# A mixture-of-experts layer with its second shared products moved, a 14-slot weight ring, and expert rows scattered into a table by token and choice

## The chip, the core and the metric

One core of a Trainium2 chip runs one program. The metric is the device time of one execution in microseconds. TensorE (PE) multiplies, VectorE (DVE) and ScalarE (ACT) work element by element, GpSimd (POOL) does so too and issues the indirect transfers, and SyncE (SP) issues the plain transfers. All transfers run on the core's 16 DMA engines.

## What is computed

The input x is 32 x 32 x 512, read as 1024 tokens (rows) of 512. Two layers are added to it, one after the other; the change touches the first and the seam between them.

```python
# first layer
xt = einsum(x, weights[condition])                # a 32x32 mix per batch row -> 1024 x 512
scores = softmax(xt @ router_w + router_b) + router_bias
idx = top 2 experts of 16, within the best 2 groups of 4
gate[t, idx] = scores[t, idx]
y = sum over e of gate[:, e] * ((silu(xt@w1[e]+b1[e]) * (xt@w2[e]+b2[e])) @ w3[e] + b3[e])
z = (silu(xt@sw1+sb1) * (xt@sw2+sb2)) @ sw3 + sb3  # shared expert, 256 wide
x = x + y + z
# second layer
u = causal convolution of x over time, one 512-tap kernel per channel, length mask
h = relu(u @ up_w)**2 @ down_w                     # 512 -> 1024 -> 512
r = ((u @ fc1_w) @ expert_w * (sum of the top 2 of u @ gate_w)) @ fc2_w
x = x + layernorm(h + r) * ln_gamma + ln_beta
```

## The kernel before

The 1024 rows are NT = 8 tiles of 128. Products that need full precision are split in a high and a low half (three matmuls each, `split3`, L400 to L407). Every engine has one hand-written instruction stream, and semaphores tie them together; there is no scheduler, so the order in the code is the order on each engine.

**Front.** The mix (PE L1279) goes through the staging buffer `xstage` (four tiles, ACT L641), from which ACT stores the mixed rows to DRAM as `xrow` (L645). The router (PE L1291, a long DVE chain from L879) picks two experts per token, and DVE gives each (token, choice) pair a slot in a sorted order in which each expert's rows begin a new block of 128: 2048 pairs in NB = 31 blocks of 128, so 1920 of the 3968 places are padding. `tokx` (DVE L986, from 16 small one-hot matmuls, PE L1358) lists the token of each place. Meanwhile PE does the first shared products (`shared_products`), ACT and DVE make `hid` and split it.

**Second shared products** (PE L1369 to L1388). For each of the 8 tiles: one product of `gt` and `b3m` (the biases b3, L1379) and six of `hidh`, `hidl` with `swh`, `swl`. DVE adds the result to `acc` (`add_y`, L917). They stand ahead of the blocks.

**Blocks** (PE loop from L1398). Block n: 16 matmul records (8 products) of `xt` with the weights in `ew` (L1405), then the second product of block n-2 (`block_y`, L1394), then the transposes of block n+2 (L1365). POOL gathers the block's rows from `xrow` with `tokx` into `xg` (L560, four buffers). DVE copies the result to `yout` (L1101, four buffers), and SP stores it to `ysort` in DRAM (L474). Expert weights (768 KB each) stand in `ew`, 16 slots: experts 0 to 7 are loaded from the front on (SP waits for `wsel_in` only), 8 to 15 once the second shared products are through (`y_done`), and blocks 16 to 30, whose experts are known only at run time, take slots 0 to 14 anew, loaded after the store of block 0 to 14. The Toeplitz pieces `toep` of the convolution are loaded over freed slots from SP's step 23 on. In the middle of the gathers POOL does 15 small operations for the convolution kernel (L572 to L586, after DVE's powers L1077) and the store of that kernel `kpad` (L592 to L594).

**Combine.** POOL waits for all stores, then gathers the expert rows of each token and choice, 16 indirect transfers of 128 rows into `yg` (L606), by `sloti`. DVE multiplies by `gk` and adds to `acc` (L1154, 16 of them), PE transposes each finished tile (L1449), ACT copies it to `u_t` (L752). PE's product of `ewt` and `fc2raw` (L1441) stands ahead of the transposes. POOL adds `bet` to `acc` tile by tile (L613).

**Second layer.** Convolution (L1461), turned back (L1470), gate logits (L1291), up and down products (L404 to L406), and at the end for each of the last four tiles: DVE statistics (L1183, L1184), ACT square root (L779), DVE reciprocal and `nmr` (L1189, L1190), ACT normalise (L784), DVE times `gam` and plus `acc` (L1199, L1201), SP store (L493).

## Time and profile before

| | |
|---|---|
| median of 3 runs | 416.92 us (415.62 to 421.37) |
| profiled execution | 415.92 us, of which the span from first to last instruction is 413.9 us |
| PE busy | 343.5 us (83% of the span) |
| DVE busy | 182.1 us (44%) |
| ACT busy | 119.7 us (29%) |
| POOL busy | 93.7 us (23%) |
| moved by DMA | 67.85 MB |

A busy share is an average over stages. The front lasts to about 64 us, the second shared products to 92 us, the blocks to 209 us, the combine to 254 us and the second layer to the end.

### The profile page before, as it was taken

The page shows a single profiled execution, that of the slowest core. Times are in us where ns is not written, and L with a number is a line of the kernel's source. Part 1 is how long each engine was busy: PE and PEld are TensorE (multiplying, and loading weights), DVE is VectorE, ACT ScalarE, POOL GpSimd, SP SyncE. Part 2 cuts the span into 40 slices and gives each one's busy share as a digit, 9 for nine tenths or more (in the row PEclk, how much of TensorE's full clock was granted, in tenths as well). Part 3 has the DMA queues.
Part 4 walks back from the last instruction along what each step waited for, and adds up shares of the span by engine and source line. Part 5 has one row for each costly group of instructions (what it writes and reads, how often), then busy time and mean ns, then how long its engine had stood idle before and what let it go on. Part 6 is the DMA issues. An engine that isn't in the chain of part 4 may idle for free.

```text
span 413.9 us, 5243 instructions
## 1 busy us (share of the span) xinstructions
PE 343.5 (83%) x1883; PEld 248.5 (60%) x1883; DVE 182.1 (44%) x354; ACT 119.7 (29%) x199; POOL 93.7 (23%) x124
## 2 busy tenths in 40 slices
PE   8668999999969499799962316986999899999991
PEld 3235785568858488688721202442788778788871
DVE  2235886326816232133312563691432044542256
ACT  1255312013362123223200406345322233321222
POOL 3640003013413511521007773009200000000000
PEclk9889998899988889999987555996999999999998
DMA  6699302119999996757995765600000000110002
GB/s 227 225 364 406 105 0 50 54 51 333 385 396 404 408 338 229 258 181 187 379 348 135 230 244 187 220 2 0 2 0 0 2 0 2 51 51 2 1 0 102
DMA packets 34245, 67.85 MB, mean 164 GB/s; under 512 B 4584, under 2 KB 5580, under 8 KB 34220
## 3 DMA queue, kind: packets, MB, share of 16 engines
q1 hardware_dynamic: 28348, 52.79, 35.1%
q0 software_dynamic: 4112, 12.54, 10.1%
q10 hardware_dynamic: 1760, 2.20, 1.5%
q8 instruction: 15, 0.25, 0.3%
q14 instruction: 10, 0.08, 0.1%
HBM read 55.10 MB, written 12.40 MB: 163 GB/s over the span
## 4 chain that ended last, share of the span: by engine, by line
PE 64%; DMA 15%; DVE 7%; POOL 5%; issue 4%; ACT 3%; SPq 2%; DVEq 0%; POOLq 0%; ACTq 0%
PE bank L404 12%; PE bank L406 11%; PE bank L405 11%; PE bank L1405 9%; DMA ysort<-yout 6%; PE bank L1461 5%; PE bank L1394 4%; POOL yg L606 3%; PE bank L1365 3%; DMA xg<-xrow,tokx 2%; DVE acc L1154 2%; PE bank L1291 2%; PE bank L1379 2%; DMA xrow<-xstage 2%; DMA yg<-ysort,sloti 2%
## 5 line engine op out<-in xcount | busy, mean ns | idle before, releaser
L1405 PE MATMUL bank<-xt,ew 128*128 128x128 f32 x496 | 63.8, 284 | 0.0
L1405 PEld LDWEIGHTS bank<-xt,ew 128*128 128x128 f32 x496 | 61.1, 201 | 0.7 <-issue 0.5
L560 POOL DMA_INDIRECT xg<-xrow,tokx x31 | 32.7, 1055 | 88.7 <-PE bank L1365 52.2
L1394 PE MATMUL bank<-ew,bhid 128*128 128x512 f32 x62 | 32.8, 614 | 3.3 <-DVE yout L1101 3.3
L718 ACT ACTIVATE xt<-bank 128x512 f32<-128x512 f32 x31 | 18.4, 597 | 53.2 <-PE bank L1365 49.7
L1449 PE MATMUL bank<-ident,acc 128*128 128x128 f32 x32 | 8.9, 433 | 26.1 <-DVE acc L1154 26.1
L1217 DVE TENSOR_TENSOR sq<-rel 128x512 f32<-128x512 f32 x16 | 12.1, 758 | 41.1 <-ACT rel L804 41.0
L1365 PEld LDWEIGHTS bank<-ident,xg 128*128 128x128 f32 x124 | 15.9, 146 | 23.1 <-issue 13.8
L1101 DVE COPY yout<-bank 128x512 f32<-128x512 f32 x31 | 21.4, 691 | 16.4 <-DMA ysort<-yout 14.2
L1154 DVE SCALAR_TENSOR_TENSOR acc<-yg,gk,acc 128x512 f32<-128x512 f32 x16 | 18.2, 1150 | 21.1 <-DMA yg<-ysort,sloti 20.8
L404 PE MATMUL bank<-dnh,sqh 128*128 128x512 f32 x64 | 25.2, 394 | 2.5 <-DVE sql L1225 1.6
L1365 PE MATMUL bank<-ident,xg 128*128 128x128 f32 x124 | 19.5, 283 | 7.6 <-DMA xg<-xrow,tokx 7.6
L404 PE MATMUL bank<-ah,uph 128*128 128x512 f32 x64 | 25.0, 391 | 0.0
L405 PE MATMUL bank<-al,uph 128*128 128x512 f32 x64 | 24.9, 390 | 0.0
L406 PE MATMUL bank<-dnh,sql 128*128 128x512 f32 x64 | 24.9, 390 | 0.0
L405 PE MATMUL bank<-dnl,sqh 128*128 128x512 f32 x64 | 24.9, 389 | 0.0
L406 PE MATMUL bank<-ah,upl 128*128 128x512 f32 x64 | 24.9, 389 | 0.0
L606 POOL DMA_INDIRECT yg<-ysort,sloti x16 | 16.8, 1048 | 32.8 <-DMA ysort<-yout 28.2
L1449 PEld LDWEIGHTS bank<-ident,acc 128*128 128x128 f32 x32 | 5.7, 217 | 29.7 <-DVE acc L1154 22.4
L1461 PE MATMUL bank<-toep,u_t 128*32 128x512 f32 (+3 forms) x256 | 20.2, 461 | 1.1 <-ACT u_t L752 1.1
L1109 DVE SCALAR_TENSOR_TENSOR bhid<-bank,b12d,bsil 128x128 f32<-128x128 f32 x15 | 5.3, 351 | 35.1 <-ACT bsil L730 33.2
L804 ACT ACTIVATE rel<-bank 128x512 f32<-128x512 f32 x16 | 9.6, 598 | 36.0 <-PE bank L406 35.9
(302 smaller groups left out, 617.9 us busy)
## 6 DMA issues: line engine op xcount, KB each, us to landing
ew<-in_L_ffn_ew SPq DMA_DIRECT2D x24, 512.0 KB, 11.7
ew<-in_L_ffn_ew SPq DMA_DIRECT2D x45, 256.0 KB
ysort<-yout SPq DMA_DIRECT2D x31, 256.0 KB, 6.9
toep<-kpad SPq DMA_DIRECT2D x4, 1536.0 KB, 10.9
acc<-in_x SPq DMA_DIRECT2D x4, 512.0 KB, 5.3
xrow<-xstage ACTq DMA_DIRECT2D x4, 512.0 KB, 7.2
upraw<-in_L_ffn_up_w SPq DMA_DIRECT2D x1, 2048.0 KB, 11.1
dnraw<-in_L_ffn_down_w SPq DMA_DIRECT2D x1, 2048.0 KB, 9.2
```

Source lines behind the costliest of these rows:

```text
L404: pe.matmul(dst, lh, rh, start=(start and k == 0), stop=False)
L405: pe.matmul(dst, lh, rl, start=False, stop=False)
L406: mm = pe.matmul(dst, ll, rh, start=False, stop=(stop and k == n_k - 1))
L560: pool.indirect_dma_start(xg[:, n % XGS, :], None, xrow, bass.IndirectOffsetOnAxis(ap=tokx[:, n:n + 1].bitcast(U32), axis=0))\
L606: pool.indirect_dma_start(yg[:, n % YS, :], None, ysort, bass.IndirectOffsetOnAxis(ap=sloti[:, k, i:i + 1].bitcast(U32), axis=0))\
L718: act.activation(xt[:, n % 2, :, :], bank[n % 2][:, :].rearrange("p (k n) -> p k n", k=KC), ACT.Copy)\
L1101: dve.tensor_copy(yout[:, n % YOS, :], bank[6 + n % 2][:, :]).then_inc(yout_ok, 1)
L1154: dve.scalar_tensor_tensor(acc[:, i, :], yg[:, n % YS, :], gk[:, k, i:i + 1], acc[:, i, :], ALU.mult, ALU.add).then_inc(comb_ok, 1)
L1365: mm = pe.transpose(bank[n % 2][:, k * P:(k + 1) * P], xg[:, n % XGS, k * P:(k + 1) * P], ident[:, :])
L1394: pe.matmul(bank[6 + n % 2][:, :], bhid[:, n % BHS, :], ew[:, ring(n), W3], start=True, stop=True)\
L1405: mm = pe.matmul(bank[2 + n % 2][:, w * P:(w + 1) * P], ew[:, ring(n), col + k * P:col + (k + 1) * P], xt[:, n % 2, k, :], start=(k == 0), ...
L1461: mm = pe.matmul(bank[g % 3][j * B:(j + 1) * B, 0:T - k * P], u_t[:, h0 + j, k, :], toep[:, (h0 + j) % TS, k * P:T], start=(k == 0), stop= ...
```

## The change

The second shared products go behind the blocks, with their splits and their operand sw3 (`sw3raw`, `hid`, `hidh`, `hidl` get places of their own): four tiles' products before the combine, the others each ahead of the transposes of a tile. `ew` gets 14 slots; experts 0 to 7 and 12, 13 are loaded once all of `xrow` is stored, 8 to 11 after the first shared products, the other 17 one by one. A second one-hot product gives `dstx`, which holds 2 x token + choice for each place; padding gets numbers past the end in `tokx` and `dstx`, and the transfers skip these rows. POOL scatters the rows of `yout` into `ytok` by `dstx`, seven blocks behind the gather. SP then loads tile i of `ytok` in one plain transfer for both choices. L1441's product goes behind the convolution, POOL's addition of `bet` behind its other work, and in the last four tiles DVE normalises, in `centred` and `scaled`, without ACT's normalise.

```diff
-    YS = 8
+    YS = 4
+    AHEAD = 7
+    RING = 14
-    ysort = nc.dram_tensor("ysort", [NB * P, T], F32).ap()
+    ytok = nc.dram_tensor("ytok", [N * K, T], F32).ap()
...
     def ring(n):
-        return n % E
+        return n if n < RING else n - RING if n < 2 * RING else n - 2 * RING + 8
...
+    def load_step(d):
+        return d * 7 // 5 if d < RING else d + 8
...
-        sp.wait_ge(wsel_in[1], 16 * (NT - 2))
-        for g in range(2):
-            static_pair(g)
         sp.wait_ge(tr_done, 1)
         sp.dma_start(ewraw[:, :, :], expert_w.rearrange("(a p) m -> p a m", p=P)).then_inc(ew_in, 16)
-        for g in range(2, E // 4):
-            static_pair(g)
+        sp.wait_ge(tr_done, 2)
+        for par in range(2):
+            sp.wait_ge(xrow_out[par], 16 * NT // 4)
+        for g in range(4):
+            static_pair(g, st_in[g // 2])
+        static_pair(6, st_in[2])
...
-        sp.wait_ge(y_done, NT)
-        for g in range(E // 4, E // 2):
-            static_pair(g)
+        sp.wait_ge(c_done, 2 * SH)
+        for g in range(4, 6):
+            static_pair(g, st_in[3])
...
         for n in range(NB):
             sp.wait_ge(yout_ok, n + 1)
-            sp.dma_start(ysort[n * P:(n + 1) * P, :], yout[:, n % YOS, :]).then_inc(ys_out[n % YOS], 16)
-            if n < ND:
-                dynamic_load(n)
-            g = n - (E + TS * T // WCOLS - 1)
+            for d in range(NB - RING):
+                if load_step(d) == n:
+                    load(d)
+            g = n - 19
...
+        for k in range(YOS):
+            sp.wait_ge(ys_out[k], 16 * ((NB + YOS - 1 - k) // YOS))
+        sp.wait_ge(bx_done, NB)
+        for i in range(NT):
+            wait(sp, comb_ok, K * (i - YS + 1))
+            sp.dma_start(yg[:, i % YS, :, :], ytok[i * P * K:(i + 1) * P * K, :].rearrange("(p k) t -> p k t", k=K))\
+                .then_inc(yg_in[i % YS], 16)
...
+        def scatter(n):
+            pool.wait_ge(yout_ok, n + 1)
+            pool.indirect_dma_start(ytok, bass.IndirectOffsetOnAxis(ap=dstx[:, n:n + 1].bitcast(U32), axis=0),
+                                    yout[:, n % YOS, :], None, bounds_check=K * N - 1, oob_is_err=False)\
+                .then_inc(ys_out[n % YOS], 16)
+
+        def move(lo, hi):
+            for n in range(lo, hi):
+                if n < NB:
+                    gather(n)
+                if n == AHEAD:
+                    pool.wait_ge(tok_ok, 2)
+                if n >= AHEAD:
+                    scatter(n - AHEAD)
...
-            act.activation(silu(u), bank[4 + u % 2][:, :], ACT.Silu, bias=b12[:, 0, u % 2:u % 2 + 1]).then_inc(silu_ok, 1)
+            wait(act, hid_ok, u - 1)
+            act.activation(silu[:, u % 2, :], bank[4 + u % 2][:, :], ACT.Silu, bias=b12[:, 0, u % 2:u % 2 + 1])\
+                .then_inc(silu_ok, 1)
...
+        for i in range(4):
+            add_y(i)
         for n in range(K * NT):
             i, k = n // K, n % K
...
+            if k and i + 4 < NT:
+                add_y(i + 4)
...
+        def centred(i):
...
+            dve.scalar_tensor_tensor(osum[:, i % TH, :], bank[i % TH][:, :], mv[:, i, 0:1], gam[:, :], ALU.subtract,
+                                     ALU.mult).then_inc(norm_ok, 1)
+
+        def scaled(i):
...
+            dve.scalar_tensor_tensor(acc[:, i, :], osum[:, i % TH, :], rstd[:, i:i + 1], acc[:, i, :], ALU.mult,
+                                     ALU.add).then_inc(fin_ok, 1)
...
+        pe.wait_ge(swl_ok, 3)
+        pe.wait_ge(hidl_ok, 2)
+        for i in range(4):
+            y_product(i)
         for i in range(NT):
+            if i + 4 < NT:
+                y_product(i + 4)
             pe.wait_ge(comb_ok, K * (i + 1))
-            wait(pe, u_ok, i - 5)
+            wait(pe, u_ok, i - 3)
```

How PE's stream reads between the one-hot products and the third block, before (`hidh_a` and `swh` are the operands of the second shared products; one of the eight tiles is shown):

```order
L1358 MATMUL bank<-hotb,hotp 128x32 x16
L1379 MATMUL bank<-b3m,gt 128x512
L404 MATMUL bank<-swh,hidh_a 128x512
L405 MATMUL bank<-swl,hidh_a 128x512
L406 MATMUL bank<-swh,hidl_a 128x512
```

and in the changed kernel:

```order
L1378 MATMUL bank<-hotb,hotp 128x32 x16
L1380 MATMUL bank<-hotb,hotp 128x32 x8
L1387 MATMUL bank<-ident,xg 128x128 x8
L1407 MATMUL bank<-xt,ew 128x128 x8
L1387 MATMUL bank<-ident,xg 128x128 x4
```

The transposes of blocks 0 and 1 now follow the one-hot products directly, and nothing of the second shared products stands between.

POOL's stream from its first gather on, in the changed kernel (`ytok<-yout,dstx` is the scatter; before, this place holds 14 gathers in a row and then the small operation at L572):

```order
L571 DMA xg<-xrow,tokx 128x512 x8
L578 DMA ytok<-yout,dstx 2048x512
L571 DMA xg<-xrow,tokx 128x512
L578 DMA ytok<-yout,dstx 2048x512
L571 DMA xg<-xrow,tokx 128x512
```

Eight gathers come first, then one scatter for each gather; there are 31 of each in all, and 16 gathers of `yg` are gone.

DVE's stream at the combine, in the changed kernel (L924 adds a shared product, L1157 an expert row):

```order
L924 TENSOR_TENSOR acc<-bank,acc 128x512 x4
L1157 SCALAR_TENSOR_TENSOR acc<-yg,gk,acc 128x512 x2
L924 TENSOR_TENSOR acc<-bank,acc 128x512
L1157 SCALAR_TENSOR_TENSOR acc<-yg,gk,acc 128x512 x2
L924 TENSOR_TENSOR acc<-bank,acc 128x512
```

Before, 16 of the L1154 kind stood there alone; now the eight additions of shared products are woven in, so that the addition for tile 7 stands ahead of the expert rows of tile 4.

## Rows read from the trace of the kernel before

**Rows 1.** Busy time by stretch: us, engine busy (count), clock, DMA share, GB/s
```profile
core 0: us, PE busy (x) PEld busy (x) DVE busy (x) ACT busy (x) POOL busy (x), PEclk, DMA share, GB/s
225.00:240.00 15.00, 4.69 (x18) 2.86 (x16) 6.46 (x9) 5.17 (x5) 11.80 (x12) 0.50 0.81 246
```

**Rows 2.** Chain that ended last: start us, us, what; front
```profile
core 0 of [0], span 413.9 us
...
19.03 8.41 DMA xrow<-xstage
```

**Rows 3.** Timeline of PE, front to blocks: start, us, instruction, [idle before]
```profile
28.11 1.11 PE L1264 MATMUL bank<-ident,xstage 128*128 128x128 f32 x4 [3.05 <-ACT xstage L641]
...
70.59 2.07 PE L1379 MATMUL bank<-b3m,gt 18*128 18x512 f32 x2
...
75.44 1.35 PE L1379 MATMUL bank<-b3m,gt 18*128 18x512 f32 x2
...
83.60 1.12 PE L1379 MATMUL bank<-b3m,gt 18*128 18x512 f32 x2
...
92.29 1.95 PE L1405 MATMUL bank<-xt,ew 128*128 128x128 f32 x16
```

**Rows 4.** Timeline of POOL: gathers, and the kernel's small operations
```profile
67.40 1.04 POOL L560 DMA_INDIRECT xg<-xrow,tokx  x1 [32.77 <-DVE tokx L986]
...
100.56 1.72 POOL L560 DMA_INDIRECT xg<-xrow,tokx  x1 [2.14 <-PE bank L1365]
...
130.62 0.76 POOL L572 TENSOR_SCALAR sw<-ci_k 128x16 f32<-128x16 f32 x1 [12.95 <-DVE ci_k L1077]
...
136.90 1.04 POOL L560 DMA_INDIRECT xg<-xrow,tokx  x1 [0.15 <-issue]
138.24 0.96 POOL L560 DMA_INDIRECT xg<-xrow,tokx  x1 [0.30 <-issue]
```

**Rows 5.** Timeline of PE, blocks to convolution
```profile
121.51 2.05 PE L1394 MATMUL bank<-ew,bhid 128*128 128x512 f32 x2 [3.28 <-DVE yout L1101]
...
143.03 1.11 PE L1365 MATMUL bank<-ident,xg 128*128 128x128 f32 x4 [5.36 <-DMA xg<-xrow,tokx]
143.94 3.62 PE L1405 MATMUL bank<-xt,ew 128*128 128x128 f32 x16
...
170.00 0.66 PE L1365 MATMUL bank<-ident,xg 128*128 128x128 f32 x4 [2.19 <-DMA xg<-xrow,tokx]
...
205.76 3.00 PE L1394 MATMUL bank<-ew,bhid 128*128 128x512 f32 x6
...
253.80 6.00 PE L1461 MATMUL bank<-toep,u_t 128*32 128x512 f32 x64 [1.13 <-ACT u_t L752]
```

**Rows 6.** Chain that ended last, two equal block steps on PE
```profile
182.99 1.79 PE bank L1405 x16
...
186.07 1.79 PE bank L1405 x16
```

**Rows 7.** DMA issues: what, engine, count, KB each, median us to landing
```profile
toep<-kpad SPq DMA_DIRECT2D x4, 1536.0 KB, 10.9
acc<-in_x SPq DMA_DIRECT2D x4, 512.0 KB, 5.3
```

**Rows 8.** Timeline of DVE, blocks and combine
```profile
100.49 0.96 DVE L1053 TENSOR_TENSOR angle<-dimh,lvals 128x784 f32<-128x784 f32 x1
...
211.45 0.69 DVE L1101 COPY yout<-bank 128x512 f32<-128x512 f32 x1 [3.08 <-DMA ysort<-yout]
...
221.92 0.75 DVE L1154 SCALAR_TENSOR_TENSOR acc<-yg,gk,acc 128x512 f32<-128x512 f32 x1 [9.78 <-DMA yg<-ysort,sloti]
...
241.33 10.18 DVE L1154 SCALAR_TENSOR_TENSOR acc<-yg,gk,acc 128x512 f32<-128x512 f32 x5 [3.49 <-DMA yg<-ysort,sloti]
```

**Rows 9.** Chain that ended last: a store, and the gate logits
```profile
212.17 5.60 DMA ysort<-yout
...
282.94 5.95 PE bank L1291 x16
```

**Rows 10.** Timeline of DVE, the last four tiles
```profile
399.42 0.70 DVE L1183 BATCH_NORM_STATS2 stats<-bank 128x6 f32<-128x512 f32 x1 [2.71 <-PE bank L406]
...
410.80 0.69 DVE L1201 TENSOR_TENSOR acc<-osum,acc 128x512 f32<-128x512 f32 x1
```

279 lines of the change are left out of this document (128 added, 151 removed).

## Prediction

> **What bounds the kernel now.** I read the busy time by stretch first. From 225 to 240 us PE is busy for 4.69 of 15 us, and its granted clock is 0.50 of full speed (1.2 of 2.4 GHz) [rows 1]: the combine is no PE stage. The timeline of PE gives the borders. The second shared products run up to the first block at 92.29 us, with tiles starting at 70.59 and 75.44 (4.85 us, at a low clock) and then 83.60 (three tiles in 8.16 us, 2.7 us each, at the high clock) [rows 3]. The blocks run from 92.29 to 208.76 us (205.76 + 3.00), and the convolution starts at 253.80 [rows 5]. So blocks take 116.5 us and the seam behind them 45.0 us. An undisturbed block step is 186.07 - 182.99 = 3.08 us of dense PE work [rows 6]. 31 of these are 95.5 us, so about 20 us are waits, low clock behind them, and the small work of the convolution kernel. The three large waits are named in the rows: 3.28 us for `yout`, whose store lay in SP's queue behind late weight loads, and 5.36 and 2.19 us for gathers that POOL issued late [rows 5]. In the seam the last store lands 5.60 us after 212.17 [rows 9], the first expert row is added at 221.92, and the last five additions start only at 241.33 [rows 8]: 16 indirect gathers, issued one by one, set that pace.
>
> **The change, part by part.** I follow three borders: the first block (T), the end of the last block (E), the start of the convolution (C).
>
> *Front.* ACT waited for the staging buffer until the first `xrow` store landed, 8.41 us after its issue [rows 2], and PE 3.05 us with it [rows 3]. The static weight loads that shared the engines with it are now issued after all `xrow` stores. The gain lies between 0 and the 3.05 us; another store of half the size took 5.60 us with little beside it [rows 9], so I take 2. Against this, ACT's fourth silu now needs `hid` 1 from DVE, behind the one-hot masks, and the gate transposes wait for that silu: 0.9 us by the order of the streams. Eight more one-hot products cost at most another 0.9. Before, POOL issued its first gather at 67.40 [rows 4]; with -2 + 0.9 + 0.9 it is 67.2.
>
> *First block.* Its gather used to be hidden behind the second shared products; that cover is gone. The late gather at 136.90 [rows 4] let PE go on at 143.03 [rows 5], 6.1 us later, beside weight loads, as here, where experts 8 to 11 (3 MB) are under way. Transposes and the copy to `xt` add about 1. T = 67.2 + 6.1 + 1 = 74.3 instead of 92.3, or **-18.0**. PE is idle for some 7 us in between, and may start the blocks at the low clock; 1 us for this is in the next part.
>
> *Blocks.* 116.5 us less the three waits (10.8) is 105.7. Steps behind a long wait ran slowly (3.62 us for 16 records at 143.94 where a dense step has 1.79 [rows 5, 6]); two such places cost about 5 together, which leaves 100.7 undisturbed. New waits:
> - POOL's small operations start when DVE has the powers, and take 136.90 - 130.62 = 6.3 us [rows 4]. The gather behind them is now that of block 15, wanted at the end of step 13. Powers come 2.4 us after the product of step 9, +6.3, +6.1 for the gather is 14.8; PE has work for 13.1 (three steps and most of a fourth). That is 1.7 late, 3 with a scatter in the way, and 1.5 for the clock behind it.
> - Weights. The Toeplitz pieces (1.5 MB each, 10.9 us to landing [rows 7]) are issued at SP steps 19 to 22, ahead of the weights of blocks 28 to 30. About 5.5 MB stand in the queue up to block 28's; at some 300 GB/s left beside the rows (an estimate; with 246 GB/s in [rows 1] as the low end) that is 18.4 + 2 us, against 6 steps or 18.5. 1.9 us late; block 29 waits for 2.4 MB more, 7.9 us against 5.0: another 3. Together 5, and 1.5 for the clock.
> - 1 at the start and 0.5 for small gaps.
>
> The sum is 100.7 + 4.5 + 6.5 + 1.5 = 113.2, so E = 187.5 instead of 208.8. Stores and gathers no longer stand in SP's queue, so the wait for `yout` and its clock loss are not replaced.
>
> *Seam.* PE starts the first four tiles of the second shared products as soon as `yout` is whole, E + 1. At 2.7 us each [rows 3] they end at E + 11.7. Beside them, POOL scatters block 30 (E + 1 to E + 2.3, by a gather's 1.0 and 0.3 between two [rows 4]), the store lands 5.6 later [rows 9], and SP's first plain load of 512 KB takes at most the 5.3 of [rows 7]: E + 13.2. So DVE adds tile 0 up to E + 14.8 (0.75 each [rows 8]). PE goes on with a shared tile and four transposes, 3.1 us a round, and ends the eighth tile at about E + 24. DVE adds it (0.7) and only then the expert rows of tiles 4 to 7, 8 times 0.75 and small gaps: E + 31. As before, where the last addition ended at 251.51 and the convolution began at 253.80 [rows 5, 8], 2.3 us follow. C = E + 33.3 instead of E + 45.0. DVE's last five additions took 2.04 us each [rows 8] while POOL added `bet`; that work of POOL comes later now, so 0.75 stands for all. C = 220.8 instead of 253.8: **-33.0** up to here.
>
> *Behind it.* PE waited 3.43 us ahead of the gate logits, which then took 5.95 us for 16 records [rows 9], 0.37 each, the pace of the low clock. L1441's product now fills that wait. It costs 0 if the high clock holds, 2 if not; the logits then take 3.7 instead of 5.95, or the same. I take -2 (kept ends: +2 and -2.2). *Last tiles.* From the first statistics at 399.42 to the last addition at 411.49 DVE works for 12.1 us [rows 10], three full-width operations (0.70, 0.68, 0.69) and small ones per tile, in part waiting for ACT. Now a tile is 0.70 + 0.75 + 0.75 and about 0.5, four are 10.8: -1.3. The second shared splits on ACT and DVE (1 to 1.3 us at steps 21 to 24) hide in steps in which either has over 1 us free. The later addition of `bet` on POOL lies beside the up products, where DVE's 0.7 us operations have slack.
>
> *Sum.* 413.9 [rows 2] - 33.0 - 2.0 - 1.3 = 377.6. The profiled execution was 2.0 longer than its span, and the median of the runs is 1.0 above it: 380.6. Since bounds of the block waits (8 us of 11 are for late weights, POOL and clock) are more likely too high than too low, with less to move for padding than a full 128 rows, I put the forecast at **379**.
>
> [...] 62 indirect issues now stand in the 31 steps. The gather at 100.56 took POOL 1.72 us instead of 0.96, and DVE had begun a 784-wide operation with two inputs in SBUF at 100.49 [rows 4, 8]. [...] By the row, a step with both issues slowed takes POOL 2 x (1.72 + 0.30) = 4.0 us against 3.08; it happens in a few steps only, and POOL runs four blocks ahead, so the sum stays.
>
> **Rivals.**
> - *POOL becomes the bound of the blocks (0.17).* No row shows an indirect transfer that skips rows, or one that writes to DRAM. Lower end: 0.96 and 0.30 as now. Upper end: 1.72 + 0.30. I take the lower, since the address list has the same 128 entries. POOL binds from 3.08 / 2 = 1.54 per issue on. At 2.02 for all, each of the 24 steps with both grows to 4.04: (4.04 - 3.08) x 24 = 23, less 8 of the waits counted above, which then vanish in it, is +15: 394.
> - *The seam at the low clock (0.13).* PE idles just before the blocks' last steps end (late weights) and its shared tiles take 4.85 instead of 2.7 [rows 3]: 8 x 2.15 = 17, of which some 5 hide behind the scatter and the first load, +12: 391.
> - *More is gained (0.10).* Weights and the gather of block 15 arrive in time and all of the 3.05 us come back: -11 - 1: 367.
> - *The move does nothing (0.04).* The shared products leave the front, but the first blocks wait for gathers one by one and for weights by as much. Against it: the static weights have 30 us of idle engines before T. It would give 400 to 410.
> - *Slower (0.02).* An issue with skipped rows costs POOL more than 2.6 us. Then each step is longer than 3.08 by over 2.1 in 24 steps, which with the longer start eats all 38 us: from 417 on. For it speaks only that no row has this form; against it, the gathers in the rows lie between 0.96 and 1.72 [rows 4].
>
> **How the numbers follow.** The forecast has 0.54; its own range, from the bounds above (0 to 3 in front, 2 to 11 in the blocks, -2.2 to +2 behind), is 371 to 386. Taking in most of the POOL and low-clock rivals above and the gain below, 368 to 393 leaves out about 0.2. Faster by over 2% means below 408.6; what a measurement of this kernel can tell from no change is about that 2%. Faster 0.94, same 0.03, slower 0.03.
>
> **What would show it.** First block product near 74 us; block steps of 3.08 us with waits at the transposes of block 15 and the weights of 28 and 29, and nowhere over 1 us else; POOL's indirect issues at 0.96 to 1.1 us; the last block end near 187; the convolution some 33 us after it, with DVE's expert additions at 0.75 us; 16 logits records in under 4 us; from the first of the last statistics to the end of DVE's work under 11 us. The forecast is wrong if POOL's busy share in the blocks is near full, if the rows' scatter lands later than 8 us after its issue, or if the shared tiles take over 4 us behind the blocks.

## The result, and the profile after

The changed kernel takes 389.04 us (median of 4 runs, 387.82 to 398.07) where the kernel before took 416.27 us (414.82 to 421.37). The ratio is 0.9351, 95% interval 0.9308 to 0.9393: faster. The profiled execution took 389.67 us with a span of 386.9 us, 27.0 shorter than the 413.9 before. Measured again on another chip, beside 11 runs of the kernel before (419.99 us), the same kernel took 379.13 us (377.88 to 380.91, ratio 0.9045, 0.8996 to 0.9095; profiled span 376.7). The two intervals do not overlap, and the place of that difference is one of the findings below. A few executions of any of these kernels run some per cent longer at a lower clock; the profiles of `shared_front`, `before_late_static` and `toep_two` are of such executions, so their spans are compared with nothing. I call the two profiled executions the first and the second profile of after.

The page of the first profile: PE, its clock and the bytes moved in 40 slices of 9.67 us, and DMA issues (count, size, median us to landing).

```profile
PE   8598996599998799991899869989999899999993
PEclk9699998599999699998899968999999999999999
GB/s 212 200 191 139 371 385 313 128 81 229 166 257 200 151 129 312 245 400 399 271 70 231 191 317 302 89 0 0 2 0 2 0 0 2 54 56 0 0 1 108
...
toep<-kpad SPq DMA_DIRECT2D x4, 1536.0 KB, 16.9
yg<-ytok SPq DMA_DIRECT2D x8, 512.0 KB, 3.3
...
xrow<-xstage ACTq DMA_DIRECT2D x4, 512.0 KB, 2.8
```

Three dips of PE matter up to the seam: the wait for the first gather (slices 7 and 8), a low clock in slice 14, and slice 19, where PE is busy for a tenth. Slices 18 and 19, ahead of and in that last dip, move 400 and 399 GB/s. The Toeplitz pieces now need 16.9 us to land, where they needed 10.9 [rows 7]. The `xrow` store needs 2.8 us, where the first needed 8.41 [rows 2].

PE's timeline in the first profile of after: start, us, instruction, idle time before it in brackets.

```profile
61.08 1.03 PE L1372 MATMUL bank<-ident,gates 128*18 128x128 f32 x8 [0.85 <-ACT silu L706]
...
126.76 0.66 PE L1387 MATMUL bank<-ident,xg 128*128 128x128 f32 x4 [1.54 <-issue]
...
174.29 0.60 PE L1387 MATMUL bank<-ident,xg 128*128 128x128 f32 x4
183.57 3.67 PE L1407 MATMUL bank<-xt,ew 128*128 128x128 f32 x16 [8.69 <-issue]
...
189.63 2.02 PE L1407 MATMUL bank<-xt,ew 128*128 128x128 f32 x16 [1.09 <-ACT xt L720]
...
194.14 2.99 PE L1393 MATMUL bank<-ew,bhid 128*128 128x512 f32 x6
198.07 1.09 PE L1443 MATMUL bank<-b3m,gt 18*128 18x512 f32 x2 [0.94 <-issue]
...
200.68 1.12 PE L1443 MATMUL bank<-b3m,gt 18*128 18x512 f32 x2
...
229.40 7.17 PE L1475 MATMUL bank<-toep,u_t 128*32 128x512 f32 x64 [1.11 <-ACT u_t L761]
...
256.15 3.60 PE L1495 MATMUL bank<-fc2raw,ewt 128*128 128x512 f32 x8
259.77 0.40 PE L1311 MATMUL bank<-ah,gwc 128*16 128x512 f32 x1
260.01 0.40 PE L1311 MATMUL bank<-al,gwc 128*16 128x512 f32 x1
```

The 8.69 us ahead of L1407 at 183.57 are put down to "issue". This L1407 is block 28's. Its own transposes were done a step earlier (those that end at 174.9 are already block 29's), and what L1407 reads besides `xt` is `ew`: this is the wait for block 28's weights. SP's timeline of the same profile shows them issued:

```profile
158.31 4.94 SPq L453 DMA_DIRECT2D toep<-kpad  x3
...
165.87 6.15 SPq L469 DMA_DIRECT2D ew<-in_L_ffn_ew  x2
172.11 0.77 SPq L471 DMA_DIRECT2D ew<-in_L_ffn_ew  x1
```

The last of the block's three loads (256 KB each) is issued by 172.9, and PE goes on 10.7 us later. No view gives their landing. In `toep_late` below, where no large load stands ahead of them, the loads of two later steps (issued from 161.0 and from 164.4) land in 3.6 to 4.9 us. Back in PE's rows, the last block ends at 197.13, the first shared tile follows at 198.07, a tile takes 2.6 us (200.68 - 198.07), and the convolution starts at 229.40. The 16 logits records start 0.24 us apart.

DVE's timeline of the same profile, the last expert additions (L1157):

```profile
221.23 5.88 DVE L1157 SCALAR_TENSOR_TENSOR acc<-yg,gk,acc 128x512 f32<-128x512 f32 x8
```

The last eight take 5.88 us, 0.74 each, and wait for nothing; before, five took 10.18 [rows 8], and below it is shown how these are shared out.

The three borders, against the forecast:

| | before | forecast | first profile | second profile |
|---|---|---|---|---|
| first block product T | 92.3 | 74.3 | 73.6 | 73.2 |
| end of the last block E | 208.8 | 187.5 | 197.1 | 187.9 |
| start of the convolution C | 253.8 | 220.8 | 229.4 | 220.2 |
| blocks, E - T | 116.5 | 113.2 | 123.6 | 114.7 |
| seam, C - E | 45.0 | 33.3 | 32.3 | 32.3 |
| C to the end | 160.1 | 156.8 | 157.5 | 156.5 |
| span | 413.9 | 377.6 | 386.9 | 376.7 |

### The profile page after: what moved, and what is told of

Its sections match the earlier page's. It is cut to its first block, busy times and chain, and to the rows that moved or that the text cites. A ratio compares the mean times of both kernels' runs of the same rounds, so it can differ in the third digit from the quotient of the medians.

```text
span 386.9 us, 5308 instructions
## 1 busy us (share of the span) xinstructions
PE 338.1 (87%) x1891; PEld 247.3 (64%) x1891; DVE 176.6 (46%) x348; ACT 115.5 (30%) x193; POOL 111.9 (29%) x140
## 2 busy tenths in 40 slices
DMA packets 32181, 60.00 MB, mean 155 GB/s; under 512 B 6422, under 2 KB 7418, under 8 KB 32156
## 4 chain that ended last, share of the span: by engine, by line
PE 67%; issue 10%; DVE 9%; DMA 7%; ACT 3%; POOL 2%; ACTq 0%; POOLq 0%; DVEq 0%
PE bank L1407 12%; PE bank L401 11%; PE bank L402 10%; PE bank L403 10%; PE bank L1393 5%; DMA xg<-xrow,tokx 4%; PE bank L1387 3%; PE bank L1475 3%; PE bank L1443 2%; PE bank L1311 2%; PE bank L1299 2%; DMA wsel<-in_L_cond_weights,cidx 2%; DVE upl L1177 1%; DVE acc L1157 1%; DMA condb<-in_itok_B 1%
## 5 line engine op out<-in xcount | busy, mean ns | idle before, releaser
L1407 PE MATMUL bank<-xt,ew 128*128 128x128 f32 x496 | 64.6, 286 | 9.8 <-issue 8.7
L1407 PEld LDWEIGHTS bank<-xt,ew 128*128 128x128 f32 x496 | 61.1, 201 | 11.4 <-issue 9.4
L571 POOL DMA_INDIRECT xg<-xrow,tokx x31 | 32.9, 1061 | 49.9 <-DVE dstx L989 34.8
L578 POOL DMA_INDIRECT ytok<-yout,dstx x31 | 33.4, 1077 | 45.8 <-DVE yout L1094 35.5
L1393 PE MATMUL bank<-ew,bhid 128*128 128x512 f32 x62 | 31.6, 595 | 0.0
L1239 DVE TENSOR_TENSOR sq<-rel 128x512 f32<-128x512 f32 x16 | 13.5, 843 | 38.7 <-ACT rel L813 38.7
L625 POOL TENSOR_TENSOR dnl<-dnraw,dnh 128x512 fp32r<-128x512 f32 x8 | 10.0, 1285 | 55.8 <-ACT dnh L777 55.8
L1475 PE MATMUL bank<-toep,u_t 128*32 128x512 f32 (+3 forms) x256 | 21.3, 483 | 1.1 <-ACT u_t L761 1.1
L813 ACT ACTIVATE rel<-bank 128x512 f32<-128x512 f32 x16 | 9.6, 599 | 34.7 <-PE bank L403 34.7
L1102 DVE SCALAR_TENSOR_TENSOR bhid<-bank,b,bsil 128x128 f32<-128x128 f32 x16 | 5.6, 350 | 30.9 <-ACT bsil L732 26.3
L1475 PEld LDWEIGHTS bank<-toep,u_t 128*32 128x32 f32 x256 | 8.2, 120 | 13.8 <-issue 11.0
## 6 DMA issues: line engine op xcount, KB each, us to landing
toep<-kpad SPq DMA_DIRECT2D x4, 1536.0 KB, 16.9
dnraw<-in_L_ffn_down_w SPq DMA_DIRECT2D x1, 2048.0 KB, 10.9
```

Of the source, the lines that this page charges most:

```text
L571: pool.indirect_dma_start(xg[:, n % XGS, :], None, xrow, bass.IndirectOffsetOnAxis(ap=tokx[:, n:n + 1].bitcast(U32), axis=0), bounds_check ...
L578: pool.indirect_dma_start(ytok, bass.IndirectOffsetOnAxis(ap=dstx[:, n:n + 1].bitcast(U32), axis=0), yout[:, n % YOS, :], None, bounds_che ...
L1239: tt(sq[:, v % 2, :], rel[:, v % 2, :], rel[:, v % 2, :], ALU.mult).then_inc(sq_ok, 1)
L1393: pe.matmul(bank[6 + n % 2][:, :], bhid[:, n % BHS, :], ew[:, ring(n), W3], start=True, stop=True)\
L1407: mm = pe.matmul(bank[2 + n % 2][:, w * P:(w + 1) * P], ew[:, ring(n), col + k * P:col + (k + 1) * P], xt[:, n % 2, k, :], start=(k == 0), ...
L1475: mm = pe.matmul(bank[g % 3][j * B:(j + 1) * B, 0:T - k * P], u_t[:, h0 + j, k, :], toep[:, (h0 + j) % TS, k * P:T], start=(k == 0), stop= ...
```

## Experiments

Theory: the change gains at T and in the seam what its parts free, and it loses in the blocks because the Toeplitz pieces stand ahead of the weights of blocks 28 to 30. Rivals: the pieces are harmless, and what is lost is POOL's issues, the gather of block 15, or the clock. All kernels compute the whole reference.

### The pieces of the Toeplitz matrix later

`toep_late`, and the same kernel again as `toep_late_again`, against the changed kernel:

```diff
-            g = n - 19
+            g = n - 24
```

> The changed kernel with the four Toeplitz loads issued at SP steps 24 to 27 instead of 19 to 22, so behind the weights of blocks 28 to 30; every byte moved stays the same. Theory (order in SP's queue): PE's wait of 8.7 us for block 28's weights and the low clock behind it (block step 28 with 3.67 us instead of 1.79, and 1.1 us ahead of block 29) go, the last block ends near 185 instead of 197 us, and the seam grows by at most 2 us because the table loads now stand behind the last pieces: 377 to 380 us. Rival (the engines are simply full, 400 GB/s from 164 to 184 us): the bytes have to pass anyway, the wait only moves to another place, and the time stays at 386 to 390 us.

> The kernel of toep_late once more (the Toeplitz pieces issued at SP's steps 24 to 27 instead of 19 to 22, nothing else), with more rounds, for its distance to the changed kernel and to see whether what set it apart comes again. Theory: 373 to 375 us; no wait of over 1 us for block 28's weights, the last block's end near 176, the product of the convolution kernel at the high clock (64 records of 219 ns), the seam some 4 us longer than in the changed kernel since the pieces share the engines with the loads of the expert rows. Rival (its gain came in part by chance, from the clock at the kernel product): the product falls to the low clock as in the changed kernel, and the run gives 377 to 379.

Measured: 373.87 us (372.57 to 377.5; ratio 0.900, 0.889 to 0.911), below the 377 to 380 expected, and 374.52 us (370.86 to 379.88; ratio 0.8933, 0.8871 to 0.8995), inside its range. SP's and PE's timelines of `toep_late_again`:

```profile
166.31 0.82 SPq L469 DMA_DIRECT2D ew<-in_L_ffn_ew  x2
...
167.73 10.55 SPq L453 DMA_DIRECT2D toep<-kpad  x4
186.06 17.39 SPq L490 DMA_DIRECT2D yg<-ytok  x8
...
173.31 1.95 PE L1407 MATMUL bank<-xt,ew 128*128 128x128 f32 x16
175.09 3.00 PE L1393 MATMUL bank<-ew,bhid 128*128 128x512 f32 x6
179.42 1.35 PE L1443 MATMUL bank<-b3m,gt 18*128 18x512 f32 x2 [1.33 <-issue]
...
183.56 1.12 PE L1443 MATMUL bank<-b3m,gt 18*128 18x512 f32 x2
```

The last expert weights are issued by 167.6, and only then the pieces. PE waits for no weights, and E is 178.1 (176.4 in the first run of it). The wait for block 28 thus comes from the pieces, as the theory has it. The seam pays part of it back: 36.5 us in the first run and 34.7 in the second, instead of 32.3. The pieces now share the engines with the loads of expert rows (median landing of `yg` 5.7 us instead of 3.3), and in the first run PE waits 2.02 us for the first expert additions. In the second run this wait is 0.34 us; there the first shared tile takes 4.14 us (183.56 - 179.42) instead of 2.6, at a granted clock of 0.53 to 0.62, and makes up most of the 2.4 us. Against the second profile of after, E is 9.8 earlier, C 7.4 and the span 6.6. That, and not the 15 us between 389.0 and 373.9 that the first comparison suggested, is the best measure of what the pieces' place is worth. It rests on one profile of each kernel. The medians say 4.6 us (374.52 against 379.13) on two chips, and the ratios 1.1 points, with intervals that all but touch (0.8995 and 0.8996).

`toep_split` issues two pieces at steps 19 and 20 and two at 25 and 26:

```diff
-            g = n - 19
-            if 0 <= g < TS // TP:
+            g = {19: 0, 20: 1, 25: 2, 26: 3}.get(n)
+            if g is not None:
```

> The changed kernel with two Toeplitz loads at SP steps 19 and 20 and two at 25 and 26. Theory (order in the queue): ahead of block 28's weights stand 3.1 MB instead of 4.7 MB of Toeplitz pieces, so these land some 4 us sooner: the wait shrinks from 8.7 to 3 to 5 us or less, and the table loads in the seam wait less than with all four pieces late: 376 to 382 us. Rival (full engines): 386 to 390 us.

Measured: 378.03 us (376.74 to 385.37; ratio 0.9048, 0.892 to 0.918), inside the expected range. Block 28 waits 2.25 us, E is 180.7; but the shared tiles now start up to 4.86 us apart (186.45, 191.31, granted clock 0.50), the seam is 39.0 and C 219.8. What was won in the blocks went into the clock of the seam. That is the rival "seam at the low clock" of the prediction, in a kernel in which it happens. It also happens in part in `gather_all` and `bet_early` below: one gap of 4.86 us between tiles and a seam of 35.3 us in both. There PE waits 0.94 us ahead of the first tile, as in the two profiles of after, where every tile is at the high clock. So this comes and goes too, and what decides it stays open.

`toep_two` issues two pieces behind the last weights, and two behind the first half of the expert rows' loads:

```diff
-            g = n - 19
+            g = n - 24
-            if 0 <= g < TS // TP:
+            if 0 <= g < 2:
...
+            if i == YS - 1:
+                for g in range(2, TS // TP):
+                    toeplitz(g * TP, g * TP, TP, g)
```

> The changed kernel with two Toeplitz loads at SP steps 24 and 25 and two behind the first four table loads of the seam. Theory: block 28 does not wait, as in toep_late (last block end near 176 us), and the table loads no longer stand behind four pieces, so the seam is again 32 to 33 us instead of 36.5: 369 to 372 us. Rival (the seam of toep_late was long for low clock, not for the loads): no better than toep_late, 373 to 375 us.

Measured: 377.55 us (376.06 to 383.38; ratio 0.9055, 0.8965 to 0.9145), where 369 to 372 were expected. In its profile block 28 does not wait, as expected, but two other things cost more than the loads could save: the small products of the convolution kernel take 8.3 us instead of 3.75 (see the last experiment), so that E is 183.3, and four shared tiles start 3.7 to 4.9 us apart, so that the seam is 40.4. The next kernel has its pieces at the same place and a seam of 32.2, as was expected here.

### The gather of block 15

`two_gather`: the kernel of `toep_two`, with the gather of block 15 issued ahead of POOL's small operations and that of block 16 directly behind them.

```diff
         move(0, 15)
+        gather(15)
...
-        move(15, 22)
+        gather(16)
+        scatter(8)
+        scatter(9)
+        move(17, 22)
```

> toep_two, and POOL issues the gather of block 15 ahead of its 15 small operations and that of block 16 directly behind them, ahead of two scatters. Theory: PE's waits for these two gathers (0.9 to 1.5 us each) go, and with them the low clock that made the small products of the convolution kernel take 8 us instead of 4 in some executions: 2 to 4 us less than toep_two. Rival (POOL is too late for the scatter of block 8, and the copies to yout wait instead): no gain or a loss of 1 to 3 us against toep_two.

Measured: 379.23 us (377.11 to 387.87; ratio 0.9122, 0.903 to 0.922). Expected were 2 to 4 us less than `toep_two`. The wait for block 15 is gone, 1.57 us stand ahead of the convolution kernel's product at 124.03 instead, and no gain is measured. Nor do these waits decide the pace of the product, as the expectation has it: in `pool_beside` PE waits 2.06 us directly ahead of it and it takes 3.75 us; here it takes 9.6. The prediction's 4.5 us for this place were too many: the second profile of after has 0.37, 0.17 and 0.50 us of waits for the gathers of blocks 15 to 17.

### The move of the shared products alone

`shared_front`: the eight shared tiles, their splits on ACT and DVE and their additions are back ahead of the blocks. Scatters into `ytok`, plain loads and the ring of 14 stay.

```diff
         pe.wait_ge(hid_ok, 2 * SH)
+        for i in range(NT):
+            y_product(i)
         transpose_x(0)
...
-        for i in range(4):
-            y_product(i)
         for i in range(NT):
-            if i + 4 < NT:
-                y_product(i + 4)
```

> The changed kernel with the second shared products and their splits and additions back ahead of the blocks; scatter, 14-slot ring, plain loads, load times and the late L1441 product are kept. Theory: the first block starts 21 us of products later less the 6.7 us in which PE waited for the first gather (hidden again), plus 2 to 3 us for splits, so near 91 us; the Toeplitz order still makes block 28 wait; the seam falls from 32.3 to about 20 to 24 us, as the store, the first load (about 10 us), 16 additions of 0.75 us and 2.3 us remain. Sum: +17 and -10, 394 to 398 us, so the move of the shared products gives 6 to 9 us of the 27. Rival (the seam is bound by the store and the loads, not by PE): the seam stays near 30 us and the time is 401 to 405 us.

Measured: 397.61 us (394.16 to 402.36; ratio 0.9513, 0.938 to 0.965), where 394 to 398 were expected. So all that is not the move (scatter with plain loads, the ring, the times of the loads, the changes behind the seam) is worth 4.9% together, and the move another 1.6% (against the first measurement of after, with intervals that overlap) to 4.7% (against the second). How the 4.9% divide among the parts is not shown. PE's timeline of `shared_front` shows why the move gives less than the 18.7 us by which T is earlier:

```profile
72.97 2.04 PE L1399 MATMUL bank<-b3m,gt 18*128 18x512 f32 x2 [7.74 <-DVE hidl L1007]
...
106.51 2.05 PE L1421 MATMUL bank<-xt,ew 128*128 128x128 f32 x16 [0.31 <-ACT xt L726]
...
205.65 3.75 PE L1421 MATMUL bank<-xt,ew 128*128 128x128 f32 x16 [7.50 <-issue]
...
216.37 3.00 PE L1388 MATMUL bank<-ew,bhid 128*128 128x512 f32 x6
228.81 1.09 PE L1460 MATMUL bank<-ident,acc 128*128 128x128 f32 x4 [9.44 <-DVE acc L1154]
...
243.29 1.93 PE L1472 MATMUL bank<-toep,u_t 128*32 128x512 f32 x8 [1.11 <-ACT u_t L760]
```

Its seam is 23.9 us (243.29 - 219.37), against 32.3: some 8.4 us of the eight tiles' 21 are exposed there, and the rest lies in PE's idle time of the seam, of which 9.44 us are seen ahead of the first transposes. Block 28 waits here too, 7.50 us: the late weights have nothing to do with the move. The front of this kernel is no clean return to the old one: PE waits 7.74 us for DVE, whose work there ends with the splits of `hid`, and five of the eight tiles start 4.8 to 4.9 us apart, so that its first block starts at 106.5 where the expectation had 91. The profiled run took 402.36 us and the shortest 394.16, so how much of this stands in the others is not known; as far as it does, the comparison of times makes the move look better than it is.

### The front

`before_late_static`: the kernel before, with its static weight loads issued behind the last `xrow` store.

```diff
-        sp.wait_ge(wsel_in[1], 16 * (NT - 2))
-        for g in range(2):
-            static_pair(g)
         sp.wait_ge(tr_done, 1)
...
-        for g in range(2, E // 4):
+        for par in range(2):
+            sp.wait_ge(xrow_out[par], 16 * NT // 4)
+        for g in range(E // 4):
             static_pair(g)
```

> The kernel before with only the static weight loads moved: experts 0 to 7 are issued once all of xrow is stored. Theory: the first store of the staging buffer no longer shares the engines with 3 MB of weights, PE's wait of 3.05 us for the buffer goes, and the one-hot products come 2 to 3.5 us earlier; all that stands behind moves up as a whole: 412.5 to 415 us. Rival (the wait for the buffer is the store's own latency): no change, 416 to 417.5 us.

Measured: 411.63 us (409.46 to 417.47; ratio 0.9867, 0.973 to 1.0007). PE's timeline and the DMA issues:

```profile
35.28 0.68 PE L1310 MATMUL bank<-ident,ltr 32*128 32x32 f32 x8 [0.45 <-ACT ltr L678]
...
xrow<-xstage ACTq DMA_DIRECT2D x4, 512.0 KB, 2.8
```

These transposes stand at 39.21 in the kernel before, so 3.9 us come back by where the loads are issued, in a kernel that has nothing else of the change. The first block starts at 89.85 instead of 92.29, but the last one ends at 208.9 as before (208.8): in this profile the blocks take 2.6 us longer, 1.0 of it at the gather wait that was 2.19 [rows 5] and is 3.21 now. In the time it is a gain of 1.3% (412.5 to 415 us were expected), whose interval just includes none.

### DVE and POOL beside each other

`pool_beside`: the changed kernel with eight POOL additions of 128x512 more, beside DVE's last eight.

```diff
         move(22, NB + AHEAD)
+        pool.wait_ge(by_done, NB)
+        pool.wait_ge(l1_in, 16 * 7)
+        pool.wait_ge(comb_ok, 8)
+        for i in range(8):
+            wait(pool, beside_ok, i - 1)
+            pool.tensor_tensor(ycv[:, i % 2, :], fc2raw[:, 0, :], fc2raw[:, 1, :], ALU.add).then_inc(beside_ok, 1)
...
+        dve.wait_ge(beside_ok, 8)
```

> Added to the changed kernel: eight GpSimd additions of 128x512 (two SBUF inputs, result into a scratch tile that is read by nobody), started when DVE has finished its eighth expert addition, so that they lie beside DVE's last eight. In the kernel before, five of DVE's additions took 2.04 us each while GpSimd added bet. Theory (the two engines hold each other up): DVE's last eight take about 2 us each instead of 0.75, some 8 to 10 us more; the convolution starts later by as much, and the run gives 396 to 399 us. Rival (the 10.18 us before were waits for the loads of the expert rows that the trace didn't show): the additions stay at 0.75 us each, and the run stays at 389, within 0.5%.

POOL's and DVE's timelines of it:

```profile
212.71 12.98 POOL L629 TENSOR_TENSOR ycv<-fc2raw 128x512 f32<-128x512 f32 x8 [19.91 <-DVE acc L1164]
...
213.75 12.48 DVE L1164 SCALAR_TENSOR_TENSOR acc<-yg,gk,acc 128x512 f32<-128x512 f32 x8
```

DVE's eight take 12.48 us instead of 5.88, 1.56 each, and the seam is 38.8 instead of 32.3: 6.5 us, less than the 8 to 10 expected, but by the cause expected. The run took 389.11 us (386.66 to 390.76; ratio 0.9314, 0.925 to 0.938), where 396 to 399 were expected. Its time alone could not have shown this, since the first measurement of after gave 389.04 with 32.3. By the Trainium skill (SBUF — State Buffer, SBUF: two separate sides) an operation of VectorE with two inputs in SBUF and one of GpSimd that reads SBUF take turns at a shared port, each for its whole length; the trace agrees here in the main, as DVE's pace of 1.56 and POOL's of 1.62 us are nearly the same. But alone they take 0.74 and 1.24 us (`bet_early` below), together 1.98 and not 1.6, so not quite the whole of each is spent by itself.

The prediction and the expectation above read 2.04 us each from five additions of the kernel before. That is a mean of unequal ones. DVE's timeline of before from 241.3 to 242 us only, which shows the first of the five by itself, and POOL's timeline:

```profile
241.33 5.31 DVE L1154 SCALAR_TENSOR_TENSOR acc<-yg,gk,acc 128x512 f32<-128x512 f32 x1 [3.49 <-DMA yg<-ysort,sloti]
...
239.95 6.13 POOL L613 TENSOR_TENSOR acc<-acc,bet 128x512 f32<-128x512 f32 x5
```

POOL's five additions run from 239.95 to 246.08, 1.23 us each as if alone. DVE's first one starts among them and ends only at 246.64, after 5.31 us. The next two take 0.74 and 0.75 with POOL idle, the last two 1.8 and 1.6 beside POOL again. So POOL's additions in a row held a single addition of DVE until they were through, while in `pool_beside`, where POOL takes a semaphore between two, the engines alternate. Together DVE lost 10.18 - 5 x 0.74 = 6.5 us there. This is an upper bound of what leaving `bet` out of this place is worth in the seam, since no run shows the old combine without it.

`bet_early` puts the additions of `bet` back right behind the blocks:

```diff
         move(22, NB + AHEAD)
+        pool.wait_ge(ln_in, 32)
+        for i in range(NT):
+            pool.wait_ge(xt_done, i + 1)
+            pool.tensor_tensor(acc[:, i, :], acc[:, i, :], bet[:, :], ALU.add).then_inc(resid_ok, 1)
...
-        pool.wait_ge(ln_in, 32)
-        pool.wait_ge(xt_done, NT)
-        for i in range(NT):
-            pool.tensor_tensor(acc[:, i, :], acc[:, i, :], bet[:, :], ALU.add).then_inc(resid_ok, 1)
```

> The changed kernel with POOL's addition of bet back ahead of its other late work, tile by tile behind the transposes. bet arrives only after the table loads, so POOL's eight additions (1.3 us each) fall beside the last expert additions of DVE and the start of the convolution. Theory (the slow 2.04 us additions before were due to POOL reading and writing the same memory): those expert additions that overlap take about 2 us instead of 0.75, at most four of them, +1 to +5 us. Rival (they were slow for another reason, such as the transfers then under way): DVE's additions stay at 0.75 us and the time is unchanged within 1 us.

Measured: 387.23 us (384.5 to 389.91; ratio 0.929, 0.921 to 0.937). Expected were 1 to 5 us more. It tells nothing apart: POOL could start on `bet` only at 231.68, behind DVE's additions (0.74 us each as before), so the two never met. `pool_beside` was made for this reason.

### The product ahead of the logits

`m2_after`: the product of L1495 stands behind the gate logits again.

```diff
-        for a in range(LC):
-            for m in range(LC):
-                mm = pe.matmul(bank[6 + a][:, :], ewt[:, m, a * P:(a + 1) * P], fc2raw[:, m, :],
-                               start=(m == 0), stop=(m == LC - 1))
-            mm.then_inc(m2_done, 1)
...
             logits(gwc, q, bank[q][0:2 * NE1, :]).then_inc(lgt_done, 1)
+        for a in range(LC):
+            for m in range(LC):
...
```

> The changed kernel with the four products of ewt and fc2raw (L1495) behind the gate logits instead of ahead of them. Theory (they fill PE's wait for the last halves, and keep the clock): PE waits about 3.4 us again, the 16 logits records take up to 5.95 us instead of 3.6, and the products add 3.6 us: +4 to +6 us. Rival (the clock does not depend on the filled wait): the logits take 3.7 us, and the products themselves add 3.6: +3 to +3.6 us.

Measured: 392.72 us (390.14 to 394.88; ratio 0.9447, 0.935 to 0.954). PE's timeline:

```profile
259.40 0.63 PE L1311 MATMUL bank<-al,gwc 128*16 128x512 f32 x1
259.82 0.63 PE L1311 MATMUL bank<-ah,gwc 128*16 128x512 f32 x1
...
263.87 2.31 PE L1501 MATMUL bank<-fc2raw,ewt 128*128 128x512 f32 x5
```

PE waits 3.54 us ahead of the first logits record, ten of the fifteen gaps from one start to the next are 0.38 to 0.43 us (0.24 in after), and the product comes on top. From the last transposes to the end of both it is 12.8 us here (254.6 to 267.5) and 7.3 in after: 5.5 us more, inside the 4 to 6 expected. `bet_early`, measured beside it on the same chip, is 5.5 us faster in the median. From C to the end only 3.4 us of it are left (160.9 instead of 157.5), in part since the first convolution records of that profile of after took 1.2 us longer than these. The cover was real.

### The padding

`gather_all`: the gathers read all 128 rows of every block; the scatter drops the padding as before.

```diff
-        dve.tensor_scalar(tokx[:, :], bank[3][:, 0:NSLOT], float(N), None, ALU.add).then_inc(tok_ok, 1)
-        dve.wait_ge(tok_ok, 1)
+        dve.tensor_scalar(tokg[:, :], bank[3][:, 0:NSLOT], float(N), N - 1.0, ALU.add, ALU.min).then_inc(tok_ok, 1)
+        link(dve.tensor_scalar(tokx[:, :], bank[3][:, 0:NSLOT], float(N), None, ALU.add))
```

> One thing is undone: the gathers no longer skip the padding rows of a block. The index table of the gathers is clamped to the last row, so that all 128 rows of every block are read (padding slots read row N-1, whose products the scatter still drops). 2048 of 31 x 128 = 3968 rows are wanted, so up to 1920 rows of 2 KB, 3.9 MB, are moved in addition (63.9 instead of 60.0 MB). Theory (late weights at block 28 are the term that I sized too small, and bytes in the engines decide how late): some 2 MB more lie ahead of block 28's weights by then, at 300 to 400 GB/s over 100 us in which the engines are not full; the wait there grows by 0 to 3 us, and the gathers land later by up to 1 us: 390 to 394 us. [...] Rival 2: no difference within 0.5%, which says that the skipped padding was worth nothing.

Measured: 385.1 us (381.25 to 386.14; ratio 0.9199, 0.913 to 0.927), where 390 to 394 were expected. It is lower than the 0.9351 of the first measurement of after and came out on a side that no theory had. Groups of POOL's instructions, of `gather_all` and then of after: busy us, mean ns.

```profile
L572 POOL DMA_INDIRECT xg<-xrow,tokg x31 | 33.1, 1069 | 49.6 <-DVE dstx L990 34.4 <-issue 8.1 <-PE bank L1388 6.8
```

```profile
L571 POOL DMA_INDIRECT xg<-xrow,tokx x31 | 32.9, 1061 | 49.9 <-DVE dstx L989 34.8 <-issue 8.4 <-PE bank L1387 6.7
L578 POOL DMA_INDIRECT ytok<-yout,dstx x31 | 33.4, 1077 | 45.8 <-DVE yout L1094 35.5 <-issue 6.9 <-PE bank L1387 2.7
```

Skipping rows costs and saves POOL nothing (1069 and 1061 ns). 3.94 MB more are moved (63.94 against 60.00 MB), but in as many packets (32182 and 32181): what skipping saves is bytes. Block 28 waits 9.20 us, 0.5 to 1.3 more than in the profiles of after. Why was it faster, then? Its small products of the convolution kernel ran at another clock, which led to the last run.

### The changed kernel once more

> The changed kernel itself, nothing edited, once more with more rounds. So far the profiles of kernels with the pieces of the Toeplitz matrix at their old place fall into two groups: where the 64 small products of the convolution kernel ran at the low clock (8.8 us from first to last), the last block ended at 195 to 197 us; where they ran at the high clock (3.75 us, in gather_all and pool_beside), it ended at 189.7, and block 28 waited 7.5 to 9.2 us for its weights in both. Theory (the clock at that product is a matter of chance of one execution, not of the edit): the median is between 383 and 388 us, at a ratio of 0.92 to 0.933 to the kernel before, below the 0.935 of its first measurement; if the product of the profiled run is at the high clock its last block ends at 189 to 191. Rival (the index clamp of gather_all removed something real, of 4 us): ratio 0.933 to 0.937 again, and in the profile the product at the low clock and the end of the last block at 195 to 198.

Measured: the 379.13 us of the first section, below the range that the theory gave (383 to 388); the rival falls. Groups of PE's instructions for the 64 small products (first profile of after, then second), and the second's PE timeline:

```profile
L1430 PE MATMUL bank<-rim_k,lim_k 128*16 128x64 f32 x32 | 6.3, 283 | 1.1 <-issue 1.1
L1429 PE MATMUL bank<-rre_k,lre_k 128*16 128x64 f32 x32 | 6.1, 285 | 0.8 <-issue 0.8
```

```profile
L1429 PE MATMUL bank<-rre_k,lre_k 128*16 128x64 f32 x32 | 3.6, 219 | 0.0
L1430 PE MATMUL bank<-rim_k,lim_k 128*16 128x64 f32 x32 | 3.6, 219 | 0.0
...
117.59 0.66 PE L1387 MATMUL bank<-ident,xg 128*128 128x128 f32 x4 [0.37 <-DMA xg<-xrow,tokx]
...
165.80 0.60 PE L1387 MATMUL bank<-ident,xg 128*128 128x128 f32 x4
174.26 3.75 PE L1407 MATMUL bank<-xt,ew 128*128 128x128 f32 x16 [7.86 <-issue]
...
184.91 3.00 PE L1393 MATMUL bank<-ew,bhid 128*128 128x512 f32 x6
188.85 1.09 PE L1443 MATMUL bank<-b3m,gt 18*128 18x512 f32 x2 [0.94 <-issue]
```

From the first to the last of these products the first profile takes 8.8 us (127.34 to 136.12), the second 3.75 (125.45 to 129.20). The busy time by stretch in the first profile shows what happens there: us, busy time and count of PE, PEld, DVE, ACT, POOL, then granted clock, DMA share and GB/s.

```profile
126.00:128.00 2.00, 1.24 (x16) 1.08 (x17) 0.00 (x0) 0.00 (x0) 1.39 (x3) 1.00 1.00 316
128.00:130.00 2.00, 0.90 (x9) 0.34 (x7) 0.00 (x0) 0.00 (x0) 1.69 (x2) 0.75 0.76 239
130.00:132.00 2.00, 1.25 (x9) 0.83 (x10) 0.12 (x1) 0.52 (x2) 0.14 (x1) 0.50 0.45 135
132.00:134.00 2.00, 2.00 (x21) 2.00 (x20) 0.83 (x2) 0.33 (x1) 0.37 (x1) 0.50 0.00 0
```

PE first starts only 20 of the 64 products in 4 us, with gaps of 0.25 to 0.50 us that are put down to "issue", and then the granted clock is 0.50. The two profiles differ by 9.2 us at E: 0.4 at T, 1.5 up to the product, 5.0 in it, 2.4 from there to block 28 (0.8 of it the longer wait for weights), and nothing behind. The same gaps and clock stand in the profiles of `toep_two`, `two_gather`, `bet_early` and `m2_after`, which ran on one chip; they are absent from `toep_late`, `toep_split` and `shared_front` (one chip), from `gather_all`, `pool_beside` and `toep_late_again` (a third) and from the second profile of after (a fourth). So the stall goes with the chip or the hour and not with an edit. What PE lacks in those gaps no view shows: it stays open. For the same reason a difference of 1 to 3% between kernels measured on different chips is no finding by itself; above I used the borders in the profiles for it.

## Why the prediction was right or wrong

- **Front, forecast -2 with +0.9 +0.9 against it.** Direction and mechanism right, size too small. The store lands in 2.8 us, and the logits' transposes (39.21 before) stand at 35.67, 3.5 earlier, a little past the upper end of 0 to 3.05; `before_late_static` gives the same 3.9 alone. The wait for the silu is 0.85 where 0.9 was worked out. POOL's first gather is issued at 66.2 instead of 67.2.
- **First block.** 74.3 forecast, 73.6 and 73.2 measured, behind an idle wait of 6.66 us for the gather ("some 7").
- **Blocks, undisturbed part.** Right: the second profile's 114.7 us less the excess at block 28 (11.1, below), 1.0 for gathers and 1.8 at the slow first step (16 records in 3.74 us instead of 1.95) leave 100.8, where 100.7 were worked out.
- **Blocks, weights: the mis-sized term.** The place and the cause are right (`toep_late` removes it), the size is not. From the end of block 29's transposes, the last work ahead of the wait, to E it takes 22.2 us in the first and 21.5 us in the second profile (166.4 to 187.9), where the same work takes 10.4 in `toep_late`: 11.9 and 11.1 us too long, against 5 + 1.5. The step that failed is the rate. I let block 28 wait 1.9 and block 29 another 3, but block 28 waits 7.9 to 8.7 and block 29 0.5 to 1.1. From the issue of the first piece (158.3 and 148.2) to block 28's first product it takes 25.3 and 26.0 us, where my sum had 20.4. The 5.5 MB of this queue thus passed at some 215 GB/s (an estimate, 5.5 MB over these times), below my 300 and even below the low end of 246, though 400 GB/s are moved in total. SP itself is held too: issuing two weight loads behind three pieces took it 6.15 us (3.67 in the second profile) where 0.81 is usual, as at 166.31 in `toep_late_again`.
- **Blocks, gather of block 15.** 4.5 forecast with the clock behind it, 1.0 measured in the second profile and 2.5 in the first, for blocks 15 to 17 together. `two_gather` takes the wait away and gains nothing.
- **Blocks, the product of the convolution kernel.** Not in the sum: 5 us in the first profile, none in the second. In the second, 3.5 us too much for the gathers and 4.6 too little for the weights leave, with 0.4 of small ones, the blocks 1.5 us longer than forecast. In the first it is 10.4, of which 5.4 are the weights and 5.0 this product.
- **Seam.** 33.3 forecast, 32.3 in both. Scatter, store, load and additions follow the steps as they were worked out; no addition shares its time with POOL. The 2.04 us per addition from which the prediction started is a mean that hides one of 5.31, but what follows from it, 0.75 for all without POOL, came true (0.74). `shared_front` shows what the tiles cost in the seam. That all tiles ran at the high clock was luck in part: with the same wait ahead of them, `gather_all` and `bet_early` lost 3 us there.
- **Behind it.** Forecast -2 and -1.3. From the convolution's start to the end of the logits it is 34.2 us instead of 35.1, and DVE's last four tiles take 10.0 us instead of 12.1 (10.8 were forecast). Together 2.6 in the first profile and 3.6 in the second, for 3.3. The logits run in 3.7 us as said, from the first start to what follows them; the first convolution records took 7.17 us instead of 6.00, at the low clock, and gave 1.2 of it back.
- **POOL as the bound.** Did not happen: issues take 1.06 to 1.08 us on average, and POOL is busy for 35.6 of 58 us from 72 to 130. The forms that no row had shown, a gather with skipped rows and a scatter into DRAM, cost what a plain gather does. 1.54 per issue would have been needed. The slow issue of 1.72 us [rows 4] has few of its kind: the longest of the first profile's scatters takes 1.79, the mean 1.08.
- **The total.** 379 was forecast. The first measurement is 10.0 above it: 10.4 in the blocks, less 1.1 elsewhere in the span, and 0.7 in what lies around the span. At 389.04 it is outside the forecast's own range of 371 to 386. It lies within 368 to 393 only because that range was widened for POOL as the bound and for a seam at the low clock, and neither happened in this kernel; half of the excess is the slow product, which no rival had. The second measurement is 0.1 above the forecast. I don't claim it as proof: its profile has the same mis-sized term (+4.6), hidden by terms that were too high by as much (T 1.1, gathers 3.5, seam 1.0 us).

The best kernel measured is the changed one with the pieces at steps 24 to 27: 374 us, 0.893 to 0.900 of the kernel before.

## What to carry to other kernels

Before moving or adding large loads, look who stands behind them in the same queue, and count their time to landing as it is when they come three in a row, not their bytes over a rate. Work of PE that is moved into a stage in which PE waits costs only what of it is not hidden there (some 8.4 of 21 us here). A mean over merged instructions can hide one that took seven times as long: cut the window before building on it. Compare borders in the profiles, and not only medians, when runs are from different chips: the same kernel gave 0.905 and 0.935 of its predecessor.

## What the hardware showed that was not expected

- PE starts the 64 small products of the convolution kernel with gaps put down to "issue" in five profiles, 3 to 4 us long and followed by a granted clock of 0.50 (1.2 GHz). From first to last they take 8.3 to 9.6 us there, and 3.75 in the nine others.
- Eight additions of DVE beside eight of POOL with a semaphore between two: 1.56 us each instead of 0.74, and POOL's 1.62 instead of 1.24. Beside POOL's additions in a row, one of DVE's took 5.31 us and POOL's 1.23 each.
- A gather that skips padding rows takes POOL as long to issue as one that reads them all (1061 and 1069 ns) and makes as many packets.
- 1.5 MB pieces of which three are issued within 3 to 7 us land in 13.1 to 19.3 us each (medians 15.1 and 16.9) while up to 400 GB/s are moved in total, and the issuing engine itself is held: two later loads take 3.67 to 6.15 us to issue instead of 0.81.
